# Last layer's first two query batches and first score maxima moved into the third FFN, with VectorE refining and ScalarE normalising for them

## The reference

```
x = x + tanh(g_xattn[l]) * xattn_l(layernorm(x), ctx, ctx, ...)
x = x + tanh(g_ffn[l])   * ffn_l(layernorm(x), ...)        # l = 0..3
```

```
x_scale, x_fp8 = quant_fp8(x)            # needs the maximum over all of x
y = bf16(x_fp8 @ w_fp8.T * (x_scale * w_scale) + bias)
x = x + tanh(g) * y
q = layernorm(x) @ WQ                     # last layer; k, v from ctx
A = softmax(q k.T / sqrt(8) - mask * 1e9) # per head, over 77 keys
```

## Time and profile before

| | us |
|---|---|
| median of 3 runs | 854.92 |
| lowest, highest | 854.1, 855.51 |
| the profiled execution | 854.17 |
| its span, first to last instruction | 852.4 |
| TensorE matmuls busy | 649.1 (76%) |
| VectorE busy | 563.6 (66%) |
| ScalarE busy | 300.2 (35%) |
| GpSimd busy | 278.8 (33%) |

### The profile page before, as it was taken

The page is one execution under the profiler, slowest core; times in us unless marked ns, Lnnn a source line. Parts: engine busy times, 40 slices in busy tenths (PEclk is TensorE's granted clock), DMA queues, the critical chain, the costliest instruction groups (busy, mean ns, idle before and its releaser), DMA issues. The chain is left out here.

```text
span 852.4 us, 9985 instructions
## 1 busy us (share of the span) xinstructions
PE 649.1 (76%) x2926; PEld 402.6 (47%) x2926; DVE 563.6 (66%) x1441; ACT 300.2 (35%) x559; POOL 278.8 (33%) x580
## 2 busy tenths in 40 slices
PE   5678766666469999895698881148887788979997
PEld 3434324444346664463344431124344566757875
DVE  8675786987435444449566654956457798868754
ACT  3043342122213334342034450012545445535553
POOL 4301241134323022127132431321022454445453
PEclk9576996788669999799579996555988999999999
DMA  8854230000041442101415421031610133333341
GB/s 249 198 162 121 55 98 0 1 0 0 1 130 57 127 75 70 30 1 71 112 50 146 110 72 28 0 108 43 179 27 4 51 100 100 87 122 90 127 115 59
DMA packets 67989, 67.71 MB, mean 79 GB/s; under 512 B 25119, under 2 KB 48223, under 8 KB 67552
## 3 DMA queue, kind: packets, MB, share of 16 engines
q1 hardware_dynamic: 61326, 64.61, 27.4%
q10 hardware_dynamic: 6610, 2.47, 1.1%
HBM read 50.29 MB, written 17.60 MB: 80 GB/s over the span
## 5 line engine op out<-in xcount | busy, mean ns | idle before, releaser
L1117 DVE TENSOR_REDUCE mraw<-ps 128x4 f32<-128x308 f32 x256 | 115.5, 476 | 77.3 <-PE ps L1469 33.6
L718 ACT ACTIVATE PT<-ps 110x512 f32<-110x512 f32 x192 | 110.8, 596 | 142.6 <-PE ps L1497 67.9
L1469 PE MATMUL ps<-KG,QG 98*128 98x308 f32 x256 | 113.1, 483 | 46.1 <-DVE mraw L1117 28.0
L634 POOL TENSOR_TENSOR sg<-sg,cb 128x512 f32<-128x512 f32 x64 | 84.3, 1320 | 79.1 <-ACT sg L845 74.6
L1469 PEld LDWEIGHTS ps<-KG,QG 98*128 98x128 f32 x256 | 60.3, 242 | 94.0 <-DVE mraw L1117 62.4
L1497 PE MATMUL ps<-QG,KG 128*110 128x512 f32 x192 | 94.0, 511 | 7.5 <-ACT PT L718 5.1
L552 POOL TENSOR_TENSOR nt<-nhv,rs 128x4 f32<-128x4 f32 (+1 forms) x99 | 25.0, 252 | 191.0 <-DVE rs L959 185.8
L1325 DVE TENSOR_TENSOR ps<-ps,sg 128x512 f32<-128x512 f32 x72 | 50.2, 698 | 41.7 <-POOL sg L634 38.7
L1517 PE MATMUL ps<-PT,VN 128*18 128x512 f32 x512 | 72.3, 638 | 0.0
L495 POOL CAST mhl<-mraw 128x64 fp32r<-128x64 f32 x16 | 4.6, 288 | 180.6 <-DVE mraw L1117 167.1
L1497 PEld LDWEIGHTS ps<-QG,KG 128*110 128x110 f32 x192 | 35.3, 189 | 51.6 <-ACT PT L718 39.3
(11 more groups left out here) (275 smaller groups left out, 1451.4 us busy)
## 6 DMA issues: line engine op xcount, KB each, us to landing
cb<-c_parts SPq DMA_DIRECT2D x64, 256.0 KB, 3.3
QG<-q_parts SPq DMA_DIRECT2D x48, 256.0 KB, 4.0
KG<-k_parts SPq DMA_DIRECT2D x48, 154.0 KB, 3.0
q_parts<-hiT SPq DMA_DIRECT2D x14, 256.0 KB, 2.0
q_parts<-loT SPq DMA_DIRECT2D x14, 256.0 KB, 2.3
k_parts<-kmH SPq DMA_DIRECT2D x16, 154.0 KB, 2.4
k_parts<-kmL SPq DMA_DIRECT2D x16, 154.0 KB, 2.5
VN<-v_parts SPq DMA_DIRECT2D x16, 144.0 KB, 2.6
```

The source lines that it names most:

```text
L634: pool.tensor_tensor(sg[:, n % 3, :], sg[:, n % 3, :], cb[:, k % CRING, :], ALU.mult).then_inc(sc_done, 1)
L718: act.activation(PT[0:w, q % PTR, :], ps[0:w, 4 + q % 2, :], ACT.Exp, scale=SCALE[l]).then_inc(exp_done, 1)
L1117: dve.tensor_reduce(mraw[:, n % 2, i, g * HG:(g + 1) * HG], ps[:, u % 2, 0:GK].rearrange("p (h k) -> p h k", k=K), AX_X, ALU.max).then_inc ...
L1469: ins = pe.matmul(o, QG[0:KS, n % 3, g, q], KG[0:KS, n % 3, g, :], start=True, stop=l not in (1, 2))
```

## The change

Only the last layer is meant by the new `HEADS = (3,)`. Its first two turnings and projections are called inside `ffn2` instead of at the start of `attention`, on TensorE, ScalarE and VectorE alike, and so are the scores and maxima of its batch 0. Pass -1 keeps the ten units of batch 1, on its last four steps. The layer norm that feeds the last layer (norm 7 in `LN_ORDER`) is refined by VectorE right behind its statistics, in nine instructions and two for the shift -mean * rs, and applied by ScalarE with that shift and scale (`normalise_out`, which layer 0's FFN already used for another norm). GpSimd no longer refines it. The FFN functions of layers 0 to 2 are now called from `attention`, which changes no order in layers 0 to 2.

```
+HEADS = (3,)
+def units_of(l, k, c):
+    if l in HEADS and k == -1:
+        return [(1, u) for u in range(3 * c - 24, min(3 * c - 21, 10))] if c >= 8 else []
...
+        OWN = [(0, 0), (0, 1)] + [(7, b) for b in range(B)]
+        SHIFTED = [(2, b) for b in range(3)] + [(7, b) for b in range(B)]
+        BY_POOL = [m for m in LN_ORDER if m not in OWN]
...
@@ GpSimd, after attention 2
                     pool.partition_all_reduce(am[:, 2:3], am[:, 0:1], P, RMAX).then_inc(am_all, 1)
-                    for k in range(B):
-                        refine(k)
...
@@ ScalarE
+            def normalise_out(m):
+                act.wait_ge(shift_of(m), shift_count(m))
+                for i in range(m[1] * TPB, (m[1] + 1) * TPB):
+                    ins = act.activation(xn[:, i, :], x[:, i, :], ACT.Identity, bias=nsh[:, i:i + 1], scale=rs[:, i:i + 1])
+                ins.then_inc(xn_ready, 1)
...
+                        if c == 8 and k == -1 and l == 3:
+                            normalise_out((7, 3))
...
                     act.activation(x8T[:, b % 2, :], ps[:, 4, 0:256].bitcast(BF16), ACT.Copy).then_inc(x8T_ready, 1)
+                    if b >= 2:
+                        xT_one(b - 2)
+                        q_one(b - 2)
+                    if b >= 1:
+                        normalise_out((7, b - 1))
...
@@ VectorE
+            def refine_own(m):
+                b = m[1]
                 v, t, y = [w[:, b * TPB:(b + 1) * TPB] for w in (nhv, nt, rs)]
+                dve.wait_ge(stats_ready, LN_ORDER.index(m) + 1)
                 for step in range(3):
                     link(dve.tensor_tensor(t, v, y, ALU.mult))
                     link(dve.tensor_tensor(t, t, y, ALU.mult))
+                    link(dve.scalar_tensor_tensor(out=y, in0=t, scalar=1.5, in1=y, op0=ALU.add, op1=ALU.mult))
+                if m in SHIFTED:
+                    s = slice(b * TPB, (b + 1) * TPB)
+                    link(dve.tensor_tensor(nsh[:, s], mv[:, s, 0], rs[:, s], ALU.mult))
+                    dve.tensor_scalar(nsh[:, s], nsh[:, s], -1.0, None, ALU.mult).then_inc(own_shift, 1)
...
-                    if c == 9 and k == 0:
+                    if c == 9 and k == 0 and l < 3:
                         normalise_batch(2 * l, 3)
...
@@ VectorE, ffn2
                     next_input(5, b)
-                for b in range(B + 1):
-                    if b < B:
-                        if b >= 1:
-                            dve.wait_ge(x8T_ps, b)
...
-                        dve.wait_ge(x8_done, b + 1)
-                    if b >= 1:
-                        residual(b - 1)
-                    if b >= 2:
-                        normalise_batch(6, b - 2)
+                    refine_own((7, b))
+                quantised(0)
+                quantised(1)
+                residual(0)
+                quantised(2)
+                residual(1)
+                q_rest(0)
+                quantised(3)
+                residual(2)
+                q_rest(1)
+                for u in range(4 * TPB):
+                    maximum(0, u // G, u % G)
+                residual(3)
...
@@ TensorE, ffn2
                     ins.then_inc(f2_ps, 1)
+                    if b >= 2:
+                        turn_input(b - 2)
+                        queries(b - 2)
+                for u in range(4 * TPB):
+                    scores(0, u // G, u % G)
...
@@ TensorE, attention
-                if l == 3:
-                    pe.wait_ge(f2_read, B)
...
                 for k in range(-1, B + (l < 3)):
+                    if l == 3 and k == 0:
+                        pe.wait_ge(f2_read, B)
```

More of the change, by code:

```diff
@@ L723, in attention @@
                     last = B
[L724 to L730, removed]
+                if l >= 1:
+                    (ffn0, ffn1, ffn2)[l - 1](xT_one, q_one)
+                if l not in HEADS:
+                    xT_one(0)
+                    q_one(0)
+                    if l == 0:
+                        parts_out(0)
+                        kv_out(2)
+                    xT_one(1)
+                    q_one(1)
                 if l == 0:
@@ L968, in refine_first @@
                     link(dve.tensor_tensor(t, t, y, ALU.mult))
[L969 to L972, removed]
+                    link(dve.scalar_tensor_tensor(out=y, in0=t, scalar=1.5, in1=y, op0=ALU.add, op1=ALU.mult))
[3 more added lines that the diff above has]
+                    dve.tensor_scalar(nsh[:, s], nsh[:, s], -1.0, None, ALU.mult).then_inc(own_shift, 1)
             def apply(src, n, b):
-                dve.wait_ge(rstd_ready, LN_ORDER.index((n, b)) + 1)
+                if (n, b) not in OWN:
+                    dve.wait_ge(rstd_ready, BY_POOL.index((n, b)) + 1)
                 for i in range(b * TPB, (b + 1) * TPB):
@@ L1171, in amax @@
                                            AX_X, ALU.max, apply_absolute_value=True))
-                q_rest(0)
+                if l >= 1:
+                    (ffn0, ffn1, ffn2)[l - 1](q_rest, maximum)
+                if l not in HEADS:
+                    q_rest(0)
                 if l == 0:
@@ L1186, in attention @@
                     dve.memset(ps[:, 7, :], 0.0).then_inc(o_zero, 1)
-                q_rest(1)
+                if l not in HEADS:
+                    q_rest(1)
                 if l == 2:
@@ L1210, in attention, with ffn0 @@
                             amax(B - 1)
-            def ffn0():
+            def ffn0(q_rest, maximum):
                 def product(j):
@@ L1250, in ffn0, with ffn1 @@
                 residual(B - 1)
-            def ffn1():
+            def ffn1(q_rest, maximum):
                 for b in range(B):
@@ L1518, in weighted_sums @@
                                   start=s == 0, stop=s == 1, skip_group_check=True).then_inc(pv_done, 1)
-                if l == 1:
-                    pe.wait_ge(f0_done, B)
-                if l == 2:
-                    pe.wait_ge(f1_read, B)
-                if l == 3:
-                    pe.wait_ge(f2_read, B)
-                turn_input(0)
-                queries(0)
-                if l == 0:
-                    keys_and_values(2)
-                    pe.wait_ge(ld_w2, 16)
-                turn_input(1)
-                queries(1)
+                if l >= 1:
+                    (ffn0, ffn1, ffn2)[l - 1](turn_input, queries, scores)
+                if l not in HEADS:
+                    if l == 1:
+                        pe.wait_ge(f0_done, B)
+                    if l == 2:
+                        pe.wait_ge(f1_read, B)
+                    turn_input(0)
+                    queries(0)
+                    if l == 0:
+                        keys_and_values(2)
+                        pe.wait_ge(ld_w2, 16)
+                    turn_input(1)
+                    queries(1)
                 if l == 0:
@@ L1574, in attention, with ffn0 @@
                         weighted_sums(3, 1, 1)
-            def ffn0():
+            def ffn0(turn_input, queries, scores):
                 pe.wait_ge(y_done, B)
@@ L1632, in ffn0, with ffn1 @@
                             down(i)
-            def ffn1():
+            def ffn1(turn_input, queries, scores):
                 pe.wait_ge(ld_ffn1, 48)
@@ L1658, in ffn1, with ffn2 @@
                         xn_transposed(3, b + 1)
-            def ffn2():
+            def ffn2(turn_input, queries, scores):
                 pe.wait_ge(w8_done, 1)
```

71 lines of the change are left out of this document (36 added, 35 removed).

## The result

| | us |
|---|---|
| after, median of 20 runs | 857.55 |
| before, median of 20 runs beside them | 854.05 |
| ratio, 95% interval | 1.0044, 1.0022 to 1.0065 |
| the profiled execution after | 860.3 (before: 854.17) |
| its span | 858.5 (before: 852.4) |

A ratio is that of the means of the runs, without those over 1.5% above the fastest of their kernel, and so not quite the ratio of the medians beside it. The change makes the kernel slower by 0.44%. That is outside the forecast range, and on the other side of the time before than the sum of -0.7 us.

The account below looks back on a forecast made before the run. No engine bounds the whole; VectorE is nearly always last in the changed stretch. Idle -6.3, normalising -3.1, prefilled banks -0.7 and refinement +8.8 gain 1.3 us; collision +0.6 leaves -0.7, so 854.2 us, range 852.3 to 856.3.

Parts of the forecast that it names:

- Refinement on VectorE: Third FFN: eleven instructions per batch, 2.2 us, four batches cost VectorE 8.8 us; GpSimd's removed instructions give nothing back.
- What now collides: GpSimd's split, mask row and key rows now run beside residual 3; costs 0 to 2.4 us, taken as 0.6.
- the way to the first maximum: From the third FFN's first quantisation to batch 0's first maximum on VectorE, forecast to start at 566.0.
- the two waits: VectorE idles 1.1 us before each of the first and second queries; 2.2 of 8.5 us idle stay.
- 16 maxima: Batch 0's maxima on VectorE in the last layer take 9.3 us, against 9.64 in the profile before.
- collision: GpSimd's rows beside VectorE's last residual and refinement slow the refining chain or make it wait; 0.6 us taken.
- the ten maxima: Batch 1's maxima on VectorE, behind the last residual, take 6.0 us against 6.30 before, ending at 586.8.
- the full banks: Both banks are full when each group of maxima starts, saving about one wait each, 0.7 us together.
- Rival 2: The four refining chains cost 0.326 us per instruction beside GpSimd: 4.8 us slower, some 859.7; chance 0.10.
- Rival 1: TensorE's clock rises early, during the first scores, so maxima go faster: gain 2.6 us, some 852.3; chance 0.10.
- Rival 3: The hand-over gains nothing: query waits 0.35 us longer each or collision at its upper bound; 854.9 to 856; chance 0.20.
- Rival 4: The collision costs nothing and query waits are shorter than counted: gain 1.3 to 2.5 us, some 853.0; chance 0.18.

Follow-up runs that it names:

- run 1: Kernel after plus one tiny elementwise GpSimd instruction right behind its reduction over all partitions; 852.42 us, ratio 0.9981 to before.
- run 3: Kernel before plus one more GpSimd reduction, into an unread column, behind its four refinements; 862.90 us, ratio 1.0098 to before.
- after, again: The kernel after, unchanged, timed a second time beside other runs; 855.87 us, ratio 1.0025 to before.
- run 7: Kernel after, but GpSimd refines norm 7, VectorE's order is chosen for that, and VectorE refines norm 6's last batch; ratio 0.9867 to before, again 0.9909.
- run 8: Kernel before, with only norm 6's last batch refined by VectorE instead of GpSimd; 849.75 us, ratio 0.9977 to before.
- run 9: Kernel after plus early GpSimd instruction, norm 7's last refinement moved into VectorE's long wait, norm 6's last batch refined by VectorE; 846.91 us, ratio 0.9934 to before.
- run 6: Kernel after plus early GpSimd instruction, norm 7's last refinement moved into VectorE's long wait; 849.75 us, ratio 0.9929 to before.

## Why the prediction was wrong

**The step that failed** is in "Refinement on VectorE": "GpSimd's 48 removed instructions give nothing back, because nobody waited for them." It put their removal at nothing, and it cost a wait of 3.37 us. It counted what the removed instructions took, and not what they covered. They stood first behind the reduction, and with them went the cover of a 7 us delay. A second sentence let it pass, in "What now collides": "nothing that it makes is needed before k = 0". The turning of the maxima stands ahead of batch 1's ten scores on TensorE, so the split was needed in pass -1. Runs 1 and 3 show both: without the exposed delay the change's stretch is 1.1 us shorter than before's, and with it exposed even the kernel before is 6.9 us longer in the stretch.

The delay was in the trace of before, with both its prices, and could have been read there. An earlier reduction, over the FFN's weight, stands in the attention ahead of the third FFN. The timeline of GpSimd in the kernel before:

```profile
433.30 0.38 POOL L594 PARTITION_ALL_REDUCE am<-am  x1 [5.61 <-issue]
440.60 0.70 POOL L484 TENSOR_TENSOR kmH<-kcH,cst 128x308 fp32r<-128x308 f32 x1 [6.92 <-issue]
```

The reduction of the third FFN itself stood 5.84 us behind nothing but "issue", and the listing had the configuration rows of both kernels. The Trainium skill (GPSIMD Engine Reference, 2.1 Instruction dispatch) also says that the first call to a freshly loaded GpSimd routine pays some 6 us with no instruction of its own in the profile, and to budget for it. The 5.5 to 6.5 us ahead of the reductions agree. The way back to elementwise work, which did the damage here, took 6.7 to 7.8.

**The sum without it was near, in part by luck.** Term by term, measured in the profile after: the way to the first maximum 33.57 us (forecast 34.2, the two waits being 0.80 and not 1.1); 16 maxima 9.15 (9.3); the last residual and refinement 5.5 (5.45), no collision, because GpSimd's rows came some 3 us too late to meet it; the unforeseen wait 3.37; the ten maxima 6.28 (6.0), so the full banks saved nothing there. In run 1, where the collision takes place, it cost 0.66 us, against the 0.6 taken, and that is luck: the prediction had it in the refining chain, where all eleven instructions kept their 0.197 us, and it came in two instructions of the statistics. VectorE's addition (578.50 to 579.25) had started ahead of GpSimd's mask row (578.75), and it was the mask row that took longer, 1.57 us in place of 1.21. That run's stretch gained 1.1 us, against a forecast of 0.7.

**The rivals.** Rival 2 (contended small instructions) is excluded: 0.197 us each, in three of the four chains beside nothing and in the fourth too. Rival 1 (the clock up early) didn't happen: the profile shows the lower level, 0.50, from 537 to 605, and 16 maxima at 1.2 us a pair. Rival 3 had longer waits for the queries; they were shorter. Rival 4 had shorter waits and no collision, and both came (0.6 us), but the exposed delay took back more.

**What the profile doesn't explain.** The stretch is 1.5 to 1.6 us longer, the runs are 3.1 us longer (mean of 32 runs after 857.62, of 86 before, with the same runs left out as from the ratios, 854.51). A run's time goes with its mean granted clock: pooled over all kernels here, each about its own mean, 5.4 us less for each 0.01 more. The runs after had 0.8295 on the mean and those before 0.8325. That goes with 1.6 us, and the other 1.5 are the size of the stretch's loss. The runs timed together speak for this: "after, again" and the 29 runs of before beside it had the same mean clock, 0.8303, and there the kernel after was 1.6 us longer (857.67 against 856.07), as the stretch is. Whether the lower clock elsewhere comes from the change or from which runs were drawn isn't shown. The two profiles of the kernel after speak for chance: the clock rose 11 us behind the stretch in one and 7 in the other, as in before's. Here are both, by stretches of 2 us (us, PE busy, clock, DMA share, GB/s), from the first profile and then from "after, again":

```profile
603.00:605.00 2.00, 2.00 (x9) 0.50 0.51 182
605.00:607.00 2.00, 2.00 (x10) 0.54 0.56 178
```

```profile
592.00:594.00 2.00, 2.00 (x4) 0.50 0.00 0
594.00:596.00 2.00, 1.59 (x7) 0.73 0.41 152
596.00:598.00 2.00, 2.00 (x18) 1.00 0.35 123
```

## What to carry to other kernels

Ask of each removed instruction not only who waited for it, but what it covered: the first one behind a change of state pays for that state, and when it goes, the next in the order pays, wherever it stands. Idle time put down to "issue" on an engine is a price with no instruction, and it is worth following through the program's order to every other place where the same pair of kinds of instruction meet. The word alone doesn't prove it: in before, 13.49 us of "issue" stand ahead of a split's first instruction at 615.19, and end 0.12 us behind VectorE's last maximum (615.07), so that was a wait whose releaser the profile didn't name. The configuration record at the line tells the two apart. When a stream's work is taken off one engine, the next thing in its queue (here the split, on GpSimd and through the turning on TensorE) is to be followed to whoever stands behind it.

## What the runs showed of the hardware

- GpSimd was idle 5.5 to 6.5 us ahead of a reduction over all partitions that followed elementwise work at once, and 6.7 to 7.8 us ahead of the first TENSOR_TENSOR behind such a reduction, with no releaser in the profile. This holds for both reductions of the kernel in all thirteen profiles, where nothing else covered the time. The way back cost the same directly behind the reduction (7.14, run 1) as behind 44 us of idleness and a CAST (7.20, after). The CAST in between started at once, and left the price to the TENSOR_TENSOR (after, "after, again", run 3).
- The configuration instruction goes out when the one before it on GpSimd is done, and doesn't wait for the semaphore of the instruction that it serves (513.0 against 524.8 us in run 7). So its time was hidden by ending the elementwise work earlier (runs 7, 8 and 9), and by one tiny instruction of the coming kind (runs 1, 6 and 9).
- Two small VectorE instructions took 0.53 and 0.56 us in place of 0.17 beside GpSimd's key rows (runs 1, 6 and 9), where GpSimd's mask row took 1.57 or 1.58 us in place of 1.21 beside VectorE.
